# One block's score maxima taken singly through the entropy stage, with the value banks' PReLU a step later

## The reference, cut to what matters

```python
# layer 0, per image: q, k have 24 rows, v has 192
q = prelu(conv1x1(x, w1, b1), a1); k = prelu(conv1x1(x, w2, b2), a2); v = prelu(conv1x1(x, wa, ba), aa)
score = softmax(einsum('bnc,bcm->bnm', q, k), axis=2)   # 4096 x 4096
out = einsum('bnm,bmc->bnc', score, v)
# layer 1, per channel, for lower = x - 0.5 and upper = x + 0.5
for i in range(4):                                      # widths 1, 3, 3, 3, 1
    logits = einsum('cij,cjn->cin', softplus(ms[i]), logits) + bs[i]
    if i < 3: logits = logits + tanh(fs[i]) * tanh(logits)
sign = -sign(lower + upper)
likelihood = maximum(abs(sigmoid(sign * upper) - sigmoid(sign * lower)), 1e-6)
```

## Time and profile before

| | |
|---|---|
| median of three runs (lowest, highest) | 5094.5 us (5088.8, 5107.15) |
| the profiled execution: its own time, its span | 5108.31 us, 5106.5 us |
| mean granted TensorE clock | 0.972 |
| PE busy | 4488.0 us (88%) |
| DVE busy | 4293.0 us (84%) |
| ACT busy | 3604.4 us (71%) |
| POOL busy | 970.7 us (19%) |
| DMA, mean over the span | 55 GB/s |

### The profile page before, as it was taken

How to read it: one execution, slowest core, us unless ns; L and a number is a source line. 1 busy time by engine, 2 the same in 40 slices (tenths; PEclk the granted TensorE clock), 3 DMA queues, 4 the chain that set the end, 5 groups by cost and what they waited for, 6 DMA issues and landing times.

```text
span 5106.5 us, 106238 instructions
## 1 busy us (share of the span) xinstructions
PE 4488.0 (88%) x38408; PEld 2989.5 (59%) x38408; DVE 4293.0 (84%) x5570; ACT 3604.4 (71%) x3912; POOL 970.7 (19%) x943
## 2 busy tenths in 40 slices
PE   4999879997799978999789997899978998799976
PEld 2788327773377723777247762577615785167831
DVE  4898789977999779997889968899688996889967
ACT  1666776668766687666876668766786667866687
POOL 5000411104111040111401113011231103211014
PEclk8999999999999999999999999999999999999999
DMA  2100430114310143001420114200241102410133
GB/s 49 38 20 21 102 94 19 32 34 100 85 29 22 36 110 77 26 26 38 115 69 22 30 45 113 61 25 27 59 114 46 32 23 69 106 47 26 32 82 93
DMA packets 154988, 280.17 MB, mean 55 GB/s; under 512 B 37442, under 2 KB 37826, under 8 KB 152707
## 3 DMA queue, kind: packets, MB, share of 16 engines
q1 hardware_dynamic: 154434, 272.94, 21.4%
HBM read 205.49 MB, written 50.33 MB: 50 GB/s over the span
## 4 chain that ended last, share of the span: by engine, by line
PE 42%; DVE 25%; issue 17%; ACT 10%; POOL 2%; DMA 2%; SPq 1%; DVEq 1%; ACTq 0%; POOLq 0%
PE ps L1302 7%; PE ps L1304 7%; PE ps L1306 7%; DVE mxp L999 6%; PE ps L1254 5%; DVE th L938 5%; PE ps L1093 5%; DVE arena L994 5%; ACT th L661 4%; DVE mxp L984 2%; ACT arena L654 2%; PE ps L1179 2%; ACT arena L622 2%; PE ps L1165 2%; PE ps L1137 1%
## 5 line engine op out<-in xcount | busy, mean ns | idle before, releaser
L1302 PE MATMUL ps<-v_sb,arena 128*128 128x193 f16 x8192 | 2019.0, 246 | 10.6 <-DVE arena L994 10.6
L1304 PE MATMUL ps<-v_sb,arena 128*128 128x192 f16 x8192 | 2028.0, 248 | 0.0
L1306 PE MATMUL ps<-v_sb,arena 128*128 128x193 f16 x8192 | 2011.2, 246 | 0.0
L619 ACT ACTIVATE arena<-ps 128x1024 f16<-128x1024 f32 x1024 | 1049.6, 1025 | 964.7 <-PE ps L1093 964.5
L994 DVE TENSOR_TENSOR arena<-arena 128x1024 f16<-128x1024 f32 x1024 | 1317.1, 1286 | 244.8 <-ACT arena L622 244.3
L999 DVE TENSOR_REDUCE mxp<-ps 128x1 f32<-128x512 f32 x1792 | 1171.5, 685 | 49.7 <-PE ps L1254 40.5
L938 DVE SCALAR_TENSOR_TENSOR th<-th,gates,ps 128x1024 f32<-128x1024 f32 x768 | 950.8, 1275 | 192.0 <-ACT th L661 188.3
L622 ACT ACTIVATE arena<-ps 128x1024 f32<-128x1024 f32 x1024 | 1046.4, 1022 | 0.0
L661 ACT ACTIVATE th<-ps,biases 128x1024 f32<-128x1024 f32 x768 | 824.7, 1115 | 203.4 <-PE ps L1165 164.5
L1304 PEld LDWEIGHTS ps<-v_sb,arena 128*128 128x128 f16 x8192 | 795.3, 97 | 261.9
L1302 PEld LDWEIGHTS ps<-v_sb,arena 128*128 128x128 f16 x8192 | 792.5, 97 | 143.6 <-issue 19.5
(11 more groups left out here) (120 smaller groups left out, 3545.7 us busy)
## 6 DMA issues: line engine op xcount, KB each, us to landing
x<-x2d SPq DMA_DIRECT2D x1152, 64.0 KB, 2.4
arena<-x2d SPq DMA_DIRECT2D x768, 64.0 KB, 2.5
xp<-x_dram SPq DMA_DIRECT2D x18, 1536.0 KB, 13.0
shared<-x_dram SPq DMA_DIRECT2D x64, 384.0 KB, 3.7
x2d<-shared SPq DMA_DIRECT2D x64, 384.0 KB, 3.0
res<-x2d SPq DMA_DIRECT2D x96, 256.0 KB
out_dram<-res SPq DMA_DIRECT2D x96, 256.0 KB
kst<-shared SPq DMA_DIRECT2D x32, 256.0 KB, 5.2
```

The source lines that it names most:

```text
L619: act.activation(e_hi[:, q % 4, :].rearrange("p (k n) -> p k n", k=2), sc, ACT.Exp)
L1302: pe.matmul(acc, eh, v_sb[:, m, 0:C + 1], start=(m == 0 and t % 2 == 0), stop=False, skip_group_check=True)
L1304: pe.matmul(acc[:, 0:C], eh, v_sb[:, m, VW:VW + C], start=False, stop=False, skip_group_check=True)
L1306: ins = pe.matmul(acc, el, v_sb[:, m, 0:C + 1], start=False, stop=(m == MT - 1), skip_group_check=True)
```

## The change

`FIRST_AT` goes from 22 to 11 and the groups are gone: tile m of the first block's maxima belongs to step 11 + m, for steps 11 to 42. PE takes it in the new function `first_max`, between `first_layer(s)` and `second_layer(s-1)`; it waits for the reduction of tile m - 2, which used the same bank. DVE reduces one bank, 512 columns, at the end of each of these steps. `split_max` stands at step 43 (before: 39), `turn_max` at 44 (41), `rows_out` at 45 (42). SP issues the ten stacks two at a time in the rounds v = 2 to 6. ACT's `negative`, DVE's `value` and POOL's copies of a value bank move one step back (bank s + 5 in step s, for s = 1 to 10), while PE's matmuls keep their step.

```diff
-FIRST_AT = 22
-FIRST_GROUPS = MAXES // 2
+FIRST_AT = 11
...
-                        if proj and 2 <= v < 2 + 2 * STACK_DMAS:
-                            stack((v - 2) // STACK_DMAS, (v - 2) % STACK_DMAS)
+                        if proj and 2 <= v < 2 + STACK_DMAS:
+                            for k in (2 * v - 4, 2 * v - 3):
+                                stack(k // STACK_DMAS, k % STACK_DMAS)
...
-                    if proj and s + V_LEAD < VB:
-                        values(s + V_LEAD)
+                    if proj and s >= 1 and s - 1 + V_LEAD < VB:
+                        values(s - 1 + V_LEAD)
...
-                            dve.wait_ge(max_mm, pj(BLOCKS * MAXES, 2 * g + 2))
-                            dve.tensor_reduce(mxp[:, 2 * g // BLOCKS, 2 * g % BLOCKS:2 * g % BLOCKS + 2],
-                                              ps[:, 0:2, :], AX_X, ALU.max).then_inc(max_red, 2)
+                            dve.wait_ge(max_mm, pj(BLOCKS * MAXES, m + 1))
+                            dve.tensor_reduce(mxp[:, m // BLOCKS, m % BLOCKS:m % BLOCKS + 1], ps[:, m % 2, :], AX_X,
+                                              ALU.max).then_inc(max_red, 1)
...
+                def first_max(m):
+                    if m == 0:
+                        pe.wait_ge(val_ready, pj(BANKS, BANKS))
+                    if m in (0, BLOCKS // 2):
+                        pe.wait_ge(stacks_in[m // (BLOCKS // 2)], pj(STACK_DMAS * 16, STACK_DMAS * 16))
+                    if m >= 2:
+                        pe.wait_ge(max_red, pj(BLOCKS * MAXES, m - 1))
+                    pe.matmul(ps[:, m % 2, :], qst[:, m // BLOCKS * P:(m // BLOCKS + 1) * P],
+                              kst[:, m % BLOCKS * N:(m % BLOCKS + 1) * N], start=True, stop=True).then_inc(max_mm, 1)
...
                 for s in range(SLOTS + 2):
+                    if l is not None and s < SLOTS:
+                        first_layer(s)
+                    if proj and 0 <= s - FIRST_AT < MAXES:
+                        first_max(s - FIRST_AT)
                     if l is not None:
-                        if s < SLOTS:
-                            first_layer(s)
                         if 1 <= s <= SLOTS:
                             second_layer(s - 1)
```

More of the change, by code:

```diff
@@ L704, in phase_a @@
                                 halves(l, u)
-                    if proj and s + V_LEAD < VB:
-                        negative(QK + s + V_LEAD)
+                    if proj and s >= 1 and s - 1 + V_LEAD < VB:
+                        negative(QK + s - 1 + V_LEAD)
                 if proj:
@@ L977, in phase_a @@
                             result(l, s // 4 - 2)
[L978 to L979 removed]
+                    if proj and s >= 1 and s - 1 + V_LEAD < VB:
+                        value(QK + s - 1 + V_LEAD)
                     if proj:
[L981 to L986 removed]
+                        m = s - FIRST_AT
+                        if 0 <= m < MAXES:
+                            dve.wait_ge(max_mm, pj(BLOCKS * MAXES, m + 1))
+                            dve.tensor_reduce(mxp[:, m // BLOCKS, m % BLOCKS:m % BLOCKS + 1], ps[:, m % 2, :], AX_X,
+                                              ALU.max).then_inc(max_red, 1)
+                        if m == MAXES:
                             split_max(pj(BLOCKS, 0), pj(BLOCKS * MAXES, 0))
[L988 removed]
+                        if m == MAXES + 2:
                             rows_out(pj(BLOCKS, 0), 0, l is None)
@@ L1228, in phase_a @@
                             value_bank(s + V_LEAD)
-                        g = s - FIRST_AT
-                        if 0 <= g < FIRST_GROUPS:
-                            if g == 0:
-                                pe.wait_ge(val_ready, pj(BANKS, BANKS))
-                                for i in range(2):
-                                    pe.wait_ge(stacks_in[i], pj(STACK_DMAS * 16, STACK_DMAS * 16))
-                            else:
-                                pe.wait_ge(max_red, pj(BLOCKS * MAXES, 2 * g))
-                            for m in (2 * g, 2 * g + 1):
-                                pe.matmul(ps[:, m % 2, :], qst[:, m // BLOCKS * P:(m // BLOCKS + 1) * P],
-                                          kst[:, (m % BLOCKS) * N:(m % BLOCKS + 1) * N], start=True, stop=True
-                                          ).then_inc(max_mm, 1)
-                        if g == FIRST_GROUPS + 3:
+                        if s == FIRST_AT + MAXES + 1:
                             turn_max(pj(BLOCKS, 0), 0)
```

6 lines of the change are left out of this document (removed).

## The result

| kernel | median (lowest to highest), us | span, clock of the profiled execution |
|---|---|---|
| before | 5099.31 (5088.8 to 5107.15), 5 runs | 5106.5 us, 5108.31 in all |
| changed | 5068.54 (5067.8 to 5074.03), 5 runs | 5066.2 us, 5067.95 in all, clock 0.978 |

The ratio of the runs is 0.9944, with a 95% interval of 0.993 to 0.9957: 29 us faster, where the forecast had 64. The direction was right. The size was less than half, and 5068.54 lies just beyond the upper end of the range, 5068.

A forecast was written before the change was run, and what follows sets the result against it. It took DVE to set the pace at the maxima, steps 28 to 37. Seven images at -7.2 us (-50.4) and -13.5 once made -64: 5108.3 to 5044 profiled, 5031 from the median; range 5006 to 5068.

The forecast's parts named there:

- the seam: Steps 10 and 11, tenth value bank meets first maximum: 0.4 on ACT, 0.5 waiting for `value`, 0.3 for POOL's copies.
- The base of 46.24: Steps 10 to 21: the last image's 46.24 us, plus 1.8 for three reductions behind `result` and the seam, together 49.2.
- its sign of failing as a whole: Steps 10 to 21 growing by more than 4 us an image, the price of all work placed in idle time.
- the 14 us that I took off: Whole kernel: median of the runs shown, 5094.5, is 14 below the profiled 5108.3, so 5044 became 5031.
- the 4.6 that steps 22 to 27 were to win: Steps 22 to 27 fall from 28.34 to 23.7 us an image, partly by losing waits for stacks, 2.6 an image.
- 28 to 37: Steps 28 to 37: single reductions cost 0.60 instead of 1.14 a step, four steps take 13.2; -5.3 us an image.
- B: Rival: steps 28 to 37 gain nothing, as ACT, PE's layers and PSUM pairs need as long; 5068 us, chance 0.14.
- D: Rival: reductions behind `result` cost nothing and the later PReLU wins 1 us in steps 0 to 9; 5007, chance 0.13.
- Steps 38 to 48: End of the image: five more reductions, 3.0 us, against 3.8 of DVE idle time; +0.6 us an image.
- the first stage: Stage without layer 1: single tiles in two banks overlap, 0.74 us a tile, 37.20 becomes 23.7; -13.5 once.
- C: Rival: two stacks a round delay side loads by 3 us beyond their cover in each image; 5052 us, chance 0.15.
- E: Rival: the tile ahead of PE's second layer costs each of 32 steps 0.38 us; 5116 us, chance 0.08.

The follow-up runs named there:

- e2: Changed kernel with the first block's maxima starting at step 12 instead of 11: 5065.8 us, ratio 0.9944.
- e5: Kernel before with only Relu, PReLU and copies of a value bank one step later: 5113.48 us, ratio 1.003.
- e3: Changed kernel with PE's matmul of the maxima behind the second layer instead of ahead of it: 5055.97 us, ratio 0.9925.
- e7: Changed kernel with POOL's copies of a value bank behind its work for the units in each step: 5039.99 us, ratio 0.9881.
- e1: Changed kernel with Relu, PReLU and copies of a value bank back in the step of its matmuls: 5047.26 us, ratio 0.9912.
- e4: Kernel before with only the ten stacks issued two in a round, rounds 2 to 6: 5084.41 us, ratio 0.9983.
- e8: Changed kernel with value banks' parts back in their matmuls' step and POOL's copies behind its work for the units: 5033.92 us, ratio 0.9869.
- e6: Kernel before with single tiles of the maxima only in the stage without layer 1: 5083.06 us, ratio 0.997.
- e9: e8 with DVE's `result` moved from the end of step 4u + 8 to the head of step 4u + 12: 5083.85 us, ratio 0.9968.

## Why the prediction was wrong

**The step that failed** is the seam in steps 10 to 21, "the tenth value bank is now in step 10 (0.4 on ACT), and `first_max(0)` waits for its `value` [...] I take 0.5, and POOL's copies of it hold up `signs` (0.3)". All three were seen, the sum of 1.2 was too small: steps 10 and 11 grew by 11.5 - 8.7 = 2.8. The bank in step 10 by itself costs 2.2 (e2) to 2.4 (e5, steps 9 to 11), against 0.4 + 0.3. The 0.4 on ACT is about right (in image 2 step 10 goes from 4.62 to 5.00 in e5). POOL's copies were sized wrongly: in e5 step 11 grows from 4.08 to 5.89, with `halves` waiting 1.70 for POOL. The copies hold up `signs` not for their own 1.43 us alone but for the `value` that they wait for as well: 2.67 us from ACT's sign to `signs`, in the changed kernel and in e5. That can't cost 0.3 when nothing covers it. The price stood in the trace of before: in image 0, steps 6 and 7, where a bank meets a unit's sign in the same way, `signs` starts 2.68 us after ACT's sign, and step 7 takes 6.27 us where the last image has 4.08, 2.2 more. I used that meeting only as cover (the wait of 1.76 for POOL in the earlier trace rows). ACT's sign and POOL's `signs` there, in the kernel before:

```profile
572.60 0.63 ACT L627 ACTIVATE lu_sign<-lu_sign 128x512 f32<-128x512 f32 x1 [0.27 <-POOL lu_sign L516]
```

```profile
575.91 1.27 POOL L521 TENSOR_TENSOR lu<-lu,lu_sign 128x512 f32<-128x512 f32 x1
```

PE's wait was sized well as long as POOL's path runs beside it: 0.6 by e2 and e3, against 0.5. With POOL's path cut (e7) steps 10 and 11 are still 1.5 above those of e1.

The base of 46.24 was a little low too. Without the bank steps 10 and 11 take 8.6 (e1) and in the last image 7.9, and not for stacks: with the stacks out of these rounds (e4) they still take 8.7, and with POOL's copies behind its work for the units step 10 falls from 4.6 to 3.4 to 3.7 (e8). The 1.5 us that I called side loads late behind stacks were in part POOL's chain once more. The whole stretch, steps 10 to 21, grew by 52.6 - 47.7 = 4.9 us in image 0, the image I worked with, and by 3.7 in the mean. The prediction had named growth of more than 4 us as its sign of failing as a whole.

The ten steps behind the seam took 41.0, where the forecast had 38.3 (the last image's) and 1.8, 0.9 less. The step times show where it is. Steps 12 to 15 take 4.32, 4.30, 3.47 and 4.08, where the last image has 3.72, 3.77, 3.84 and 4.08: a cycle pays 0.75 and not 0.60, and pays 1.13 of it in its first two steps, of which the third gives 0.37 back. Steps 12 to 21 are two cycles and such a first half, 2 x 0.75 + 1.13 = 2.6 where 1.8 was forecast.

**The second error** is the 14 us that I took off to get from the profiled execution to the median, and the choice of image 0. Against the profile the forecast was 5044 and the result 5067.95, 24 over, which is the size of the miss in steps 10 to 21: 7 x (52.5 - 49.2) = 23. Against the median it was 37 over, those 24 and the 14 taken off. The images of e6 have the very instructions of before, and in its profiled execution they took 190.6 us instead of 193.4, with steps 22 to 27 at 25.1 instead of 27.8. What differs most is the wait for stacks, 18.5 us in the earlier trace rows, and in e6:

```profile
  DMA qst<-shared: 4.7, 4
```

So part of the 4.6 that steps 22 to 27 were to win belonged to that one execution, and not to the kernel's usual run. How large a part stays open, since the two profiled executions lie on either side: before's is 8 to 15 us above its four medians here, e6's 5071.72 is the lowest of its eleven runs, 11 below their median. Halfway between them, an estimate, steps 22 to 27 usually take 26.5, and the change wins 2.7. The changed kernel has no such wait: its images took 188.8 to 189.3 us, those of before 190.3 to 195.8, and its profiled execution lies on its median (5067.95 and 5068.54), while before's lies 9 above. This is also why e4 gains 22 us by the profiles and 9 by the runs: its profiled execution lies on its median, and before's lies 15 above the median of those rounds. I had counted the removal of a varying wait at the size it had in a long execution, and had then taken the length of that execution off once more.

**What was right.** Steps 22 to 27 (23.8, forecast 23.7), 28 to 37 (35.7, forecast 35.1) with DVE busy for 35.43 of 35.69, so B (the idle time moves to other engines) is out; a cycle there is 13.5 us, not 13.2, as two of its steps take 3.11 and 3.14 instead of 2.98. That is ACT's own pace, but one of the two takes 2.98 when PE's tile stands behind the second layer (e3), so that one is owed to the tile's place. Of four reductions, 2.4 us, a cycle pays 0.75, about the one behind `result`, so D (more is hidden) is out. Its other half, a gain of the later PReLU in steps 0 to 9, is refuted: these take 42.8 with it and without it (changed, e1), and in e5 no less than before. Steps 38 to 48 (34.4, forecast 34.1) and the first stage (22.2, forecast 23.7; e6). C (stacks delay side loads) is out in the changed kernel. The totals of PE's first layer, whose wait for side loads stood at 1.11 once in the earlier trace rows, are for before, the changed kernel and e8:

```profile
L1165 PE MATMUL ps<-arena,w1s 64*64 64x512 f32 x3072 | 438.0, 639 | 99.1 <-DMA arena<-x2d 43.5 <-DVE th L938 36.9 <-DVE lu L896 8.6
```

```profile
L1176 PE MATMUL ps<-arena,w1s 64*64 64x512 f32 x3072 | 428.4, 626 | 84.5 <-DVE th L938 47.5 <-DMA arena<-x2d 11.1 <-ACT arena L654 4.8
```

```profile
L1176 PE MATMUL ps<-arena,w1s 64*64 64x512 f32 x3072 | 427.9, 625 | 113.5 <-DVE th L938 54.5 <-DMA arena<-x2d 32.8 <-ACT arena L654 5.6
```

They fall from 43.5 us to 11.1, of which the stacks' earlier rounds explain a part (26.5 in e4), and rise to 32.8 when POOL's chain doesn't cover them. E (PE's tile ahead of the second layer) is out as priced: 32 steps do not pay 0.38 each, e3 shows less than 1 us an image.

Of the change's parts, measured alone, the stacks win 9, the first stage 15, and the shift costs 15; if they add up, the changed kernel's 29 leave 20 for single tiles from step 11, which weren't measured alone. That the shift costs 45 - 29 = 16 in the changed kernel (e1) and 15 by itself (e5) speaks for it. The sign of the shift is the finding. It was in the forecast at +1.2 an image, and it is the one edit of the change that makes the kernel slower; without it the rest is worth 45 us, and with POOL's order turned as well 67.

Two slips of the prediction changed nothing: the 317.1 us of the earlier trace rows are the waits of PE's matmuls, 108.4, and of its weight loads, 208.7, which run side by side, and its chances of a faster kernel add up to 0.85, not 0.84.

## What to carry to other kernels

When an instruction is moved by one step in a software pipeline, look at the last iteration of what it belongs to: in the steady state everything keeps its distance, and at the end it meets work that it never met before. Price that meeting by the nearest place in the trace where the same two things meet already, and follow every engine's queue behind it, since two late paths side by side hide one another and the longest wait (here 4.03 us, worth 0.6) isn't the dear one. Where a profiled execution lies above the median of the runs, and the change removes a wait that varies, that wait's size in the trace may be too large for the median; a second profile of the same instructions (here 18.5 against 4.7 us) shows how much it varies, if its own place among the runs is read with it. And before work is moved into an engine's idle time, ask what the engine behind it will do meanwhile: in e9 DVE's extra time was free as long as PE kept its clock, and cost 1.4 us a cycle when it didn't.
